# A transformer block on one Trainium2 core: the second normalised input kept whole, its halves made where they are used

## What is computed

```python
h = layernorm(x) * (1 + ca) + sa
x = x + ga * attention(h)                 # causal, 16 heads, low-rank keys and values
h = layernorm(x) * (1 + cb) + sb          # "the second h"
# ffn(h):
scores = sigmoid(h @ gate_w.T)            # 16 experts
topk_score, topk_ids = top_k(scores.T, 512)
xin = h[topk_ids]
eo = (silu(xin @ gw.T + gb) * (xin @ up_w.T + up_b)) @ down_w.T + down_b
out = scatter_add(eo * topk_score)
shared = (silu(h @ sh_gate_w.T) * (h @ sh_up_w.T)) @ sh_down_w.T
x = x + gb * (out + shared)
```

## Time and profile before

| | |
|---|---|
| median of 3 runs | 1234.73 us (1232.41 to 1238.22) |
| the profiled execution's own time | 1237.99 us |
| its span in the profile | 1236.3 us |
| mean granted TensorE clock | 0.957 of full speed |
| attention | to about 457 us of the span |
| shared experts | about 457 to 640 us |
| routed experts | from there to the end |
| HBM read / written | 103.97 MB / 34.13 MB |

### The profile page before, as it was taken

One profiled execution on the slowest core, in us unless ns is written; L12 is line 12 of the kernel. 1 busy time (PEld: TensorE's weight loads), 2 busy tenths in 40 slices (PEclk: granted clock), 3 DMA queues, 4 the chain that ended last, 5 costly groups with the idle time before them and its releaser, 6 DMA issues.

```text
span 1236.3 us, 21641 instructions
## 1 busy us (share of the span) xinstructions
PE 1120.8 (91%) x7422; PEld 870.5 (70%) x7422; DVE 868.1 (70%) x2206; ACT 599.2 (48%) x1085; POOL 644.5 (52%) x680
## 2 busy tenths in 40 slices
PE   4888989898988798999779999999999999999997
PEld 3544546455555467888668888888888888888886
DVE  5687779787968725777867766677766677776662
ACT  1257757776666554322134544444544444544451
POOL 4124376574655646322326565656566656566654
PEclk9779989998989879999999999999999999999999
DMA  5836677788767634797344455444546544556531
GB/s 166 103 58 105 108 126 162 133 160 157 123 148 125 160 109 173 218 191 184 119 154 113 135 141 150 123 127 124 146 126 159 124 124 120 144 125 159 125 86 18
DMA packets 102077, 165.47 MB, mean 134 GB/s; under 512 B 18120, under 2 KB 67784, under 8 KB 99920
## 3 DMA queue, kind: packets, MB, share of 16 engines
q1 hardware_dynamic: 86544, 137.86, 46.9%
q0 software_dynamic: 14336, 25.70, 10.8%
q10 hardware_dynamic: 1088, 0.52, 0.3%
HBM read 103.97 MB, written 34.13 MB: 112 GB/s over the span
## 4 chain that ended last, share of the span: by engine, by line
PE 35%; POOL 22%; issue 18%; DMA 10%; DVE 9%; ACT 2%; SPq 2%; ACTq 0%; POOLq 0%; DVEq 0%
POOL HTl L1656 12%; PE LB L766 6%; PE MB L766 6%; PE UB L619 5%; POOL out_y L1704 4%; PE LB L508 4%; POOL XG L1663 4%; PE MB L508 4%; DMA QS<-NMx 4%; PE LB L603 3%; DVE junk L1170 3%; DMA HT<-Us 3%; PE UB L508 2%; PE XB L508 2%; DMA XT<-hD 2%
## 5 line engine op out<-in xcount | busy, mean ns | idle before, releaser
L1656 POOL TENSOR_TENSOR HTl<-HF,HTh 128x512 fp32r<-128x512 f32 x160 | 223.0, 1399 | 243.4 <-ACT HTh L976 243.1
L1170 DVE CUSTOM_DVE_ANT_0 junk<-MB,MK 128x256 bf16<-128x256 f32 (+3 forms) x512 | 220.0, 484 | 58.0 <-PE MB L578 57.0
L1567 POOL TENSOR_SCALAR_AFFINE_SELECT P<-P 128x256 f32<-128x256 f32 x256 | 102.8, 426 | 163.3 <-ACT P L916 163.3
L603 PE MATMUL LB<-QS,KS 50*128 50x256 f32 (+3 forms) x512 | 128.7, 370 | 26.6 <-DMA QS<-NMx 20.7
L914 ACT ACTIVATE P<-LB 128x768 f32<-128x768 f32 x128 | 104.0, 812 | 100.5 <-PE LB L603 100.0
L976 ACT ACTIVATE HTh<-HF 128x512 fp32r<-128x512 f32 x160 | 100.4, 627 | 89.2 <-DVE HF L1443 89.2
L1704 POOL DMA_INDIRECT out_y<-EO,IDX x64 | 106.7, 1667 | 69.2 <-DVE EO L1530 63.7
L603 PEld LDWEIGHTS LB<-QS,KS 50*128 50x128 f32 x512 | 82.9, 201 | 78.7 <-issue 42.8
L578 PE MATMUL MB<-KS,QS 48*128 48x256 f32 (+3 forms) x512 | 130.3, 369 | 7.7 <-DMA KS<-ST 3.4
L983 ACT ACTIVATE SIL<-LB,gbT 128x512 f32<-128x512 f32 x64 | 43.9, 685 | 185.3 <-PE LB L508 185.3
L766 PE MATMUL LB<-WDh,HTh 128*128 128x256 f32 x320 | 94.2, 294 | 17.5 <-POOL HTl L1656 17.5
(11 more groups left out here) (266 smaller groups left out, 3014.9 us busy)
## 6 DMA issues: line engine op xcount, KB each, us to landing
WR<-in_gw SPq DMA_DIRECT2D x16, 1024.0 KB, 7.5
WR<-in_uw SPq DMA_DIRECT2D x16, 1024.0 KB, 4.9
WR<-in_dw SPq DMA_DIRECT2D x16, 1024.0 KB, 5.5
QS<-ST SPq DMA_DIRECT2D x96, 128.0 KB, 4.5
KS<-ST SPq DMA_DIRECT2D x96, 128.0 KB, 5.4
hD<-h SPq DMA_DIRECT2D x8, 1024.0 KB, 6.8
XT<-hD SPq DMA_DIRECT2D x8, 1024.0 KB, 9.1
X<-in_x SPq DMA_DIRECT2D x8, 512.0 KB, 6.0
```

What stands on the lines that cost most here:

```text
L603: m = e.matmul(LB[:, o:o + w], KS[base:base + 50, k, j * 128:(j + 1) * 128], QS[base:base + 50, k, 128 * j:512], start=True, stop=True)
L1170: m = e.tensor_tensor_reduce(junk[:, o:o + w], MB[:, o:o + w], MK[:, 512 - w:512], 1.0, -3e38, ALU.add, ALU.max, NM[:, k // 4, 4 * (k % 4) ...
L1567: m = e.affine_select(out=dd, in_=dd, compare_op=ALU.is_ge, fill=0.0, base=0, pattern=[[0, 2], [1, 128]], channel_multiplier=-1)
L1656: e.tensor_tensor(HTl[:, slot, :], HF[i][:], HTh[:, slot, :].bitcast(F32), ALU.subtract).then_inc(g_ht, 1)
```

## The change

The second h is kept as one fp32 tensor. ScalarE's copy of the transposed bank writes it whole and is now what frees the bank and what the router waits for; VectorE's subtraction is gone. The router multiplies in fp32, with a single gate table GP. The store and the load of a batch carry 512 KB instead of 1 MB; the load lands in the second half of XT, and from there ScalarE makes the high half (`round_h`) and GpSimd the low half in place (`split_h`). ScalarE does this for batch 0 in unit 15 after head 1, and for batch b + 1 right after its part of step 1 of batch b; GpSimd in unit 15 after head 3, and ahead of its part of step 2. The load is waited for by ScalarE and no longer by PE, which waits for GpSimd.

```diff
-    hD = dram("hD", [NB, 128, 2, 2, 512])
+    hD = dram("hD", [NB, 128, 2, 512])
...
-    GPh, GPl = at("GPh", 25728, [128, 2, 240], F32R), at("GPl", 27648, [128, 2, 240], F32R)
+    GP = at("GP", 25728, [128, 2, 240])
...
-    h2 = at("h2", 81024, [128, 2, 2, 512], F32R)
+    h2 = at("h2", 81024, [128, 2, 512])
...
         def store_split(b):
-            e.wait_ge(d_h2, 2 * b + 2)
-            e.dma_start(hD[b], h2[:].bitcast(F32)).then_inc(c_h2d, 16)
+            e.wait_ge(a_h2, 2 * b + 2)
+            e.dma_start(hD[b], h2[:]).then_inc(c_h2d, 16)
...
-                    e.dma_start(XT[0][:].bitcast(F32), hD[0]).then_inc(c_xt[0], 16)
+                    e.dma_start(XT[0][:, 1].bitcast(F32), hD[0]).then_inc(c_xt[0], 16)
...
-            e.dma_start(XT[b % 2][:].bitcast(F32), hD[b]).then_inc(c_xt[b % 2], 16)
+            e.dma_start(XT[b % 2][:, 1].bitcast(F32), hD[b]).then_inc(c_xt[b % 2], 16)
...
-            free[BANK[name]] = (d_h2, 2 * b + c + 1)
+            free[BANK[name]] = (a_h2, 2 * b + c + 1)
...
-            e.wait_ge(d_h2, 2 * b + 2)
+            e.wait_ge(a_h2, 2 * b + 2)
             ps = spare(name)
-            terms3(ps[:], lambda k: GPh[:, k, o:o + 128], lambda k: GPl[:, k, o:o + 128],
-                   lambda k: h2[:, 0, k, :], lambda k: h2[:, 1, k, :]).then_inc(p_sc, 1)
+            for k in range(2):
+                m = e.matmul(ps[:], GP[:, k, o:o + 128], h2[:, k, :], start=(k == 0), stop=(k == 1))
+            m.then_inc(p_sc, 1)
...
                 if i == 0:
-                    e.wait_ge(c_xt[b % 2], 16 * (b // 2 + 1))
+                    e.wait_ge(g_xl, b + 1)
...
-            e.activation(h2[:, 0, c, :], SPARE[BANK[name]][:], ACT.Copy).then_inc(a_h2, 1)
+            e.activation(h2[:, c, :], SPARE[BANK[name]][:], ACT.Copy).then_inc(a_h2, 1)
+
+        def round_h(b):
+
+            e.wait_ge(c_xt[b % 2], 16 * (b // 2 + 1))
+            e.activation(XT[b % 2][:, 0], XT[b % 2][:, 1].bitcast(F32), ACT.Copy).then_inc(a_xh2, 1)
...
+                if u == NU - 1 and k == 1:
+                    round_h(0)
...
                 glu(n_glu(b, i) - 1, i, 0.0, 4 * (b % 2) + i, n_down(b - 2, 3) if b >= 2 else 0)
+                if i == 1 and b + 1 < NB:
+                    round_h(b + 1)
...
-        def h2T(b, c, name):
-            e.wait_ge(a_h2, 2 * b + c + 1)
-            e.tensor_tensor(h2[:, 1, c, :], SPARE[BANK[name]][:], h2[:, 0, c, :].bitcast(F32), ALU.subtract).then_inc(d_h2, 1)
...
-                    if k == 2 and old2:
-                        h2T(b - 2, 0, "h2a")
-                    if k == 4 and old2:
-                        h2T(b - 2, 1, "h2b")
...
-                    kept(e.tensor_copy(GPh[:, :, 112:128], grv))
-                    settled()
-                    e.tensor_tensor(GPl[:, :, 112:128], grv, GPh[:, :, 112:128].bitcast(F32), ALU.subtract).then_inc(d_gate, 1)
+                    e.tensor_copy(GP[:, :, 112:128], grv).then_inc(d_gate, 1)
...
-                h2T(NB - 2, 0, "h0")
-                h2T(NB - 2, 1, "h1")
...
-            if w == 9:
-                h2T(NB - 1, 0, "h2")
-                h2T(NB - 1, 1, "h3")
...
+        def split_h(b):
+
+            e.wait_ge(a_xh2, b + 1)
+            e.tensor_tensor(XT[b % 2][:, 1], XT[b % 2][:, 1].bitcast(F32), XT[b % 2][:, 0].bitcast(F32),
+                            ALU.subtract).then_inc(g_xl, 1)
...
+                    if u == NU - 1 and k == 3:
+                        split_h(0)
...
+            if kind == "glu" and i == 2 and b + 1 < NB:
+                split_h(b + 1)
```

More of the change, by code:

```diff
@@ L213, in block_program @@
         "a_s", "a_rows", "a_xh", "a_hf", "a_st", "a_v", "a_nm", "a_p", "a_us", "a_hn", "a_th", "a_h2"))
-    a_sil, a_ht, a_cut, a_xt, a_score = (sem(n) for n in ("a_sil", "a_ht", "a_cut", "a_xt", "a_score"))
-    (d_s, d_w, d_modT, d_mod, d_gate, d_mv1, d_hh, d_st, d_mx, d_nm, d_rec, d_tf, d_mv2, d_h2, d_lg) = (sem(n) for n in (
+    a_sil, a_ht, a_cut, a_xt, a_xh2, a_score = (sem(n) for n in ("a_sil", "a_ht", "a_cut", "a_xt", "a_xh2", "a_score"))
+    (d_s, d_w, d_modT, d_mod, d_gate, d_mv1, d_hh, d_st, d_mx, d_nm, d_rec, d_tf, d_mv2, d_lg) = (sem(n) for n in (
         "d_s", "d_w", "d_modT", "d_mod", "d_gate", "d_mv1", "d_hh", "d_st", "d_mx", "d_nm", "d_rec", "d_tf", "d_mv2",
-        "d_h2", "d_lg"))
+        "d_lg"))
     d_own = sem("d_own")
@@ L223, in block_program @@
         "d_hf", "d_cut", "d_tb", "d_eo", "d_top", "d_oh", "d_idx", "d_xt"))
-    (g_ks, g_fill, g_rs1, g_P, g_nf, g_hn, g_x2, g_rs2, g_h2, g_ht) = (sem(n) for n in (
-        "g_ks", "g_fill", "g_rs1", "g_P", "g_nf", "g_hn", "g_x2", "g_rs2", "g_h2", "g_ht"))
+    (g_ks, g_fill, g_rs1, g_P, g_nf, g_hn, g_x2, g_rs2, g_h2, g_xl, g_ht) = (sem(n) for n in (
+        "g_ks", "g_fill", "g_rs1", "g_P", "g_nf", "g_hn", "g_x2", "g_rs2", "g_h2", "g_xl", "g_ht"))
     g_own = sem("g_own")
@@ L1608, in pool_program @@
             e.memset(V[i][:], 1.0)
-        e.memset(GPh[:].bitcast(F32), 0.0)
-        e.memset(GPl[:].bitcast(F32), 0.0)
+        e.memset(GP[:], 0.0)
         e.memset(LG[:], 0.0).then_inc(g_fill, 1)
```

## The result

The kernel after took 1250.65 us (median of 4 runs, 1249.15 to 1257.37), the kernel before 1233.57 us on the same chip (4 runs, 1232.12 to 1238.22). The ratio is 1.0143, with an interval of 1.0112 to 1.0174: slower by 17.6 us by the ratio and by 17.1 between the medians, where 15.5 were forecast. The profiled execution of after took 1249.27 us with a span of 1247.5.

What follows compares the result with a forecast made beforehand. TensorE, 91% busy, was taken to bound the kernel, so its stops counted. Terms 1.0 + 0.7 + 6.5 + 1.5 - 0.4 + 3.7 + 2.5 = 15.5 us over the median 1234.73 gave 1250.2 us, range 1240 to 1260.

Steps and rivals of the forecast that it cites:

- attention and unit 15: Attention +1.0 us from fp32 router products less VectorE's relief; unit 15 +0.7 us for ScalarE's new copy of batch 0.
- first wait (A to B): Shared experts' first product to last output projection: ScalarE's wait for batch 1's load delays that projection, +6.5 us.
- batches 3 to 5: Shared experts, later batches: copy and subtraction between late loads and PE outweigh the halved bytes, +2.5 us together, batch 6 included.
- Batch 7 has slack: Shared experts, last batch, up to the routed stage's gate-weight load (C): no cost was counted.
- Half the bytes save 0.52 MB at 402 GB/s, 1.3 us: Batch 1's load: halving brings its landing from 474.4 to 473.1 us.
- Rule and row: First wait: one VectorE op of 0.7 us holding GpSimd's subtraction would make 7.2 us; the sum kept 6.5.
- Clock: After PE's stop of over 7 us at the last output projection: 3 us at half clock, +1.5 us.
- rival (c): Stops set off more: clock low for longer, 5 us instead of 1.5, second stop brings a fall too; 1258.2 us, chance 0.14.
- Routers: Shared experts: batch 6's router -0.4 us; batch 7's +3.7 us, 3.4 of it ScalarE's wait for batch 2's load.
- nothing there waits for the second h: Attention: PE's long waits are for row maxima by DMA (19.2 us) and VectorE's last maximum (11.4 us).
- rival (b): Not slower: removing VectorE's subtractions shortens attention's way to the maxima, -5.2 us there; 1232.6 us, chance 0.08.
- Rival (a): Shared experts: halved loads land like a lone 512 KB transfer, in 3.6 us; total +4.8 us, 1239.5 us, chance 0.14.

Runs made afterwards that it cites:

- w_wait: The kernel before with only ScalarE's wait for the next batch's load added after its part of step 1, no new work: 1.0092.
- x1: The changed kernel with batch 1's load issued ahead of the weights: 1.0066 to the kernel before.
- x4: x3 with batch 1's GpSimd subtraction moved behind the last unit's normalisation: 1.001 to the kernel before.
- x5: x4 with batch 7's GpSimd subtraction also moved one step later, away from the top-k tail: 1.002 to the kernel before.
- d_nosub: The kernel before without VectorE's sixteen subtractions for the second h, the low half zero: 1.0006.
- x3: The changed kernel with batch 1's load ahead of the weights and batch 2's ahead of the last table store: 1.0016 to the kernel before.
- d_half: The kernel before without VectorE's subtractions, with two fp32 router products and 512 KB transfers, shared experts reading the high half twice: 0.9974.

## Why the prediction was right, and where its steps were not

The median is 0.5 us from the forecast. The main mechanism, ScalarE's in-order waits for two loads, is as forecast. That the sum is this close is luck: some terms were too small, one was missing, others were too large, and they cancel. Against the two pairs of profiled executions (whose spans differ by 11.2 and 17.2 us, apart mostly by attention):

| step | forecast | first pair | second pair |
|---|---|---|---|
| attention and unit 15 | +1.7 | -8.3 | +0.6 |
| first wait (A to B) | +6.5 | +8.4 | +7.5 |
| clock, routers of batches 6 and 7 (B to batch 3) | +4.8 | +7.5 | +8.0 |
| batches 3 to 5 | +2.5 | +0.2 | -2.1 |
| batch 6 to C, "Batch 7 has slack" | 0 | +3.7 | +3.4 |
| routed experts | 0 | -0.2 | -0.1 |

**First wait: right in mechanism, mis-sized by 1 to 2 us.** The largest step that failed is "Half the bytes save 0.52 MB at 402 GB/s, 1.3 us". The load took 9.0 us for 512 KB (8.7 in the second execution) where it had taken 9.4 for 1 MB, and 8.1 were forecast: in a full queue its own bytes are not the main part of its time. That the chain of engines follows was shown by w_wait and undone by x1 and x4.

**Rule and row.** The forecast left the rule of the Trainium skill ("SBUF — State Buffer", "Who interferes with whom") out of this term, because the rows of before showed GpSimd undisturbed. The subtraction was indeed not held: 2.35 us, where 2.6 were forecast. But the two instructions behind it were slow, HTl with 1.71 and nf with 1.68 us, where 1.27 and 1.31 were forecast. VectorE then worked on two subtractions with both inputs in SBUF:

```profile
468.92 3.09 DVE L1533 TENSOR_TENSOR WDl<-WR,WDh 128x512 fp32r<-128x512 f32 x2 [0.29 <-ACT WDh L968]
```

The extra 0.8 us is near the 0.7 us that the forecast named for the rule and did not add. This agrees with the rule; no experiment took these two away. The rule came true with a larger price at the top-k tail, where the forecast had not looked for a VectorE instruction with two SBUF inputs that TensorE waits for.

**Clock: too small.** Forecast +1.5 from 3 us at the half clock. The stop of 9.45 us left TensorE at 0.50 until about 480, and the output projection alone took 2.2 us more. The fall after the second stop, which the text left out of the sum, did come in both executions of after: the row of the router of batch 7 was 3.45 us instead of 1.88. That half of rival (c) was right. It does not follow every such stop: in x1 the clock did not fall.

**Routers.** At that of batch 6 TensorE's wait fell from 1.57 us to 0.74, by 0.83 where 0.68 was forecast. At that of batch 7 the wait was 2.65 us, forecast 3.4; ScalarE's idle time of 7.77 us and the landing of 5.3 were forecast as 8 and 5.5. The price of the fp32 products was right: at full clock two of them are four instructions of 0.59 us, 0.43 apart. The sum counts only seven of the eight routers: that of batch 5 runs after attention, and its 0.33 us was left out.

**Batches 3 to 5: too large.** ScalarE did wait for those loads, for example

```profile
542.10 1.06 ACT L950 ACTIVATE XT<-XT 128x1024 fp32r<-128x1024 f32 x1 [4.63 <-DMA XT<-hD]
```

but the landings came down to 13.4, 15.4 and 13.8 us (the longest was 20.0), and almost nothing of the waits reached TensorE in after. The subtraction that the forecast counted as a fixed 3.7 us between landing and TensorE mattered in another way, by holding VectorE's top-k search; that cost 3.6 us in x5. The kernel before pays for the late load itself: the 0.75 us of the earlier trace rows was about 2 us in its second execution.

**Batch 7: the step that failed.** "Batch 7 has slack" looked at the landing (3.4 us, and ScalarE did not wait) and not at what the subtraction would run beside. From batch 6 to C it is 3.4 to 3.7 us longer, of which the held product makes 2.0.

**Attention: likely of the wrong sign.** The forecast gave +1.7 us and said of its long waits that "nothing there waits for the second h". That overlooked that the halved stores shorten the waits for the row maxima, by about 6 us (below). One of the forecast's own signs of being wrong, an attention stage shorter by over 3 us, did appear in the first pair (-8.3) and not in the second (+0.6). Over all profiled executions the shared experts start at 449.4 to 458.2 us with transfers of 1 MB (five, mean 454.9) and at 446.2 to 455.2 with 512 KB (eight, mean 449.8). The means are 5 us apart and the ranges overlap, so a shorter stage is likely and not settled. In unit 15 the new copy raised TensorE's wait for the exps from 0.37 us to 0.86, so 0.5 of the forecast 0.7. VectorE's relief, the reason of rival (b), gave nothing that can be measured (d_nosub). Rival (a) fell with the landing of 9.0 us, not 3.6.

**The way out.** x3, x4 and x5 win back nearly all of the loss, and none beats the kernel before.

## What to carry to other kernels

When a tile begins to be prepared by an in-order engine, the load's landing becomes that engine's deadline for everything behind it: issue the load earlier, or put the preparation behind the work that TensorE is waiting for. Cost a moved elementwise operation also by what it will run beside: list the VectorE and GpSimd instructions of that moment that read SBUF, above all in a serial chain such as a search, where even an instruction of one element for each partition can be held for 2 us. After a long stop, look up the granted clock of TensorE's next products and count it as part of the price. And do not take one profile for a kernel: attention alone moved by 7.6 us between two executions of the kernel before.

## What the runs showed of the hardware that was not expected

**Halving large transfers shortened the waits for small ones.** The row maxima go through a 16 KB transfer on ScalarE's queue (QS<-NMx), while the stores of the second h go on SP's. TensorE's wait for it, 100 to 440 us, was 16.5 to 19.5 us in all five profiled executions with stores of 1 MB (mean 18.4) and 10.6 to 12.9 us in all eight with 512 KB (mean 12.0). One of each, both kernels run again:

```profile
PE LB L603 <- DMA QS<-NMx: 16.5, 10, 3.0
```

```profile
PE LB L604 <- DMA QS<-NMx: 12.2, 7, 2.8
```

The 6 us of waiting do not come back as 6 us of time: d_half gives about 3, and the start of the shared experts moved by 7.6 us between two executions of the kernel before.

**VectorE was held until GpSimd's instruction was done, however small its own work.** The product at L1375 took 0.69 us alone and 2.73 beside GpSimd's 2.54 us subtraction, and 0.69 again once the two were apart (x5). The instruction of one element for each partition took 2.16 us instead of 0.16 beside one of 2.58 us. This agrees with the rule named above.

**The clock after a short stop differed between kernels.** In after the second stop came 29 us after the long one and lasted 2.65 us, and the granted clock from 505 to 508 us was 0.62 on average; at the same place before it was 1.00 (window 499 to 503). In x1 TensorE had a stop of 2.53 us at the same router, after a first one of only 4.0 us, and the granted clock stayed at 1.00 (window 499 to 503 of x1):

```profile
499.81 1.99 PE L562 MATMUL XB<-h,GP 128*128 128x512 f32 x4 [2.53 <-ACT h L946]
```

So no price of the clock can be read from the length of one short stop; what decided between the two was not tested.
